# Graph attention block: softmax arguments in natural node order, a new step order, and the division of P shared by ScalarE and VectorE

## The reference

```python
h = relu(layernorm(x))
# 4 heads, then one more "back" head on the concatenated heads
Wh = h @ W[head];  f1 = Wh @ a1;  f2 = Wh @ a2
e  = leaky_relu(f1[:, None] + f2[None, :], 0.01)
e  = where(adj > 0, e, -1e9)
attn = softmax(e, axis=-1)
h_head = elu(attn @ Wh)
...
y = ffn(out) + out;  x = x + layernorm(y) * gamma + beta
h = relu(layernorm(x))
x = x + deg * (h @ Wi + b) + adj @ (h @ Wj)
```

## Time and profile before

| | us |
|---|---|
| median of 3 runs | 1514.7 (1514.22 to 1515.41) |
| profiled execution: time | 1505.55 |
| its span in the trace | 1503.5 |
| busy: TensorE matmuls | 1339.4 |
| busy: VectorE | 1190.4 |
| busy: ScalarE | 1083.5 |
| busy: GpSimd | 349.2 |

### The profile page before, as it was taken

The page is one execution under the profiler, slowest core; times in us unless marked ns, Lnnn a source line. Parts: engine busy times, 40 slices in busy tenths (PEclk is TensorE's granted clock), DMA queues, the critical chain, the costliest instruction groups (busy, mean ns, idle before and its releaser), DMA issues.

```text
span 1503.5 us, 27090 instructions
## 1 busy us (share of the span) xinstructions
PE 1339.4 (89%) x9944; PEld 1260.0 (84%) x9944; DVE 1190.4 (79%) x2833; ACT 1083.5 (72%) x2037; POOL 349.2 (23%) x234
## 2 busy tenths in 40 slices
...
DMA packets 53091, 54.07 MB, mean 36 GB/s; under 512 B 14048, under 2 KB 41696, under 8 KB 52832
## 3 DMA queue, kind: packets, MB, share of 16 engines
...
## 4 chain that ended last, share of the span: by engine, by line
PE 51%; DVE 35%; issue 6%; ACT 5%; POOL 2%; DMA 2%; POOLq 0%; ACTq 0%; DVEq 0%; SPq 0%
PE ps L747 33%; DVE arg L625 12%; PE ps L780 5%; DVE prob_lo L606 4%; DVE arg L653 4%; PE ps L830 4%; PE ps L871 4%; PE ps L840 3%; DVE elu L661 2%; DVE zneg L633 2%; DVE whx_lo L606 2%; DVE st L587 1%; POOL hx_lo L378 1%; DVE xb L699 1%; PE ps L849 1%
## 5 line engine op out<-in xcount | busy, mean ns | idle before, releaser
L378 POOL TENSOR_TENSOR hx_lo<-elu,hx_hi 128x512 fp32r<-128x512 f32 x128 | 171.2, 1338 | 622.7 <-ACT hx_hi L474 622.7
L747 PE MATMUL ps<-prob_hi,whx_hi 128*128 128x256 f32 x1024 | 298.5, 291 | 11.4 <-DVE wk L661 7.6
L747 PE MATMUL ps<-prob_lo,whx_hi 128*128 128x256 f32 x1024 | 289.7, 283 | 0.0
L747 PE MATMUL ps<-prob_hi,whx_lo 128*128 128x256 f32 x1024 | 289.2, 282 | 0.0
L625 DVE CUSTOM_DVE_ANT_0 arg<-f2bc,mask 128x512 f32<-128x512 f32 x320 | 278.7, 907 | 1.9 <-DMA f2bc<-f_rows 1.6
L444 ACT ACTIVATE arg<-arg,nmax 128x512 f32<-128x512 f32 x320 | 227.7, 718 | 0.6 <-DVE nmax L636 0.5
L440 ACT ACTIVATE arg<-arg,fcol 128x512 f32<-128x512 f32 x320 | 213.5, 721 | 12.1 <-DVE gmax L625 12.1
L780 PE MATMUL ps<-ident,arg 128*128 128x128 f32 x1280 | 186.9, 290 | 36.9 <-DVE arg L653 32.4
L747 PEld LDWEIGHTS ps<-prob_hi,whx_hi 128*128 128x128 f32 x1024 | 196.1, 192 | 17.2 <-issue 9.7
L780 PEld LDWEIGHTS ps<-ident,arg 128*128 128x128 f32 x1280 | 170.6, 209 | 45.0 <-DVE arg L653 34.8
L450 ACT ACTIVATE prob_hi<-ps 128x1024 fp32r<-128x1024 f32 x160 | 163.4, 1021 | 58.7 <-PE ps L747 33.1
...
## 6 DMA issues: line engine op xcount, KB each, us to landing
...
f_rows<-fcol SPq DMA_DIRECT2D x80, 2.0 KB, 3.4
...
```

Of the source, the lines that this page charges most:

```text
L378: pool.tensor_tensor(out=hx[1][:, 2 * c.h:2 * c.h + 2, c.u * HN:(c.u + 1) * HN], in0=elu[:, c.buf, :, :], in1=hx[0][:, 2 * c.h:2 * c.h + 2 ...
L747: i = pe.matmul(out, a, b_, start=(k == 0), stop=(k == n - 1))
```

## The change

Three things. The mask is made in natural node order by one instruction over all four row tiles; rowmax reads f2bc with a step of four floats and writes arg in natural order; turn_p reads contiguous blocks. `scale` is split: ScalarE multiplies row tile 0 of a unit (new semaphore p_scaled0, on which turn_p waits too), VectorE row tile 1. All five step tables are in a new order, in which ScalarE's has the ten new `scale` entries.

```diff
-            for n in range(NC):
-                i = dve.tensor_scalar(mask[:, n, :].rearrange("p (q c) -> p c q", c=NC), adj_f[:, n, :].rearrange("p (c q) -> p c q", c=NC),
-                                      0.0, 1.0, ALU.is_gt, ALU.mult)
-            i.then_inc(s_adj, 1)
+            dve.tensor_scalar(mask[:, :, :], adj_f, 0.0, 1.0, ALU.is_gt, ALU.mult).then_inc(s_adj, 1)
...
+            def scale(c):
+
+                act.wait_ge(rinv_made, c.unit + 1)
+                act.activation(arg[:, c.abuf, 0, :], arg[:, c.abuf, 0, :], ACT.Copy, scale=rinv[:, c.abuf, 0:1]).then_inc(p_scaled0, 1)
...
-                    dve.tensor_tensor_reduce(out=arg[:, c.abuf, n, :], in0=f2bc[:, head % F2S, :], in1=mask[:, 2 * c.u + n, :],
+                    dve.tensor_tensor_reduce(out=arg[:, c.abuf, n, :].rearrange("p (c q) -> p c q", c=NC),
+                                             in0=f2bc[:, head % F2S, :].rearrange("p (q c) -> p c q", c=NC),
+                                             in1=mask[:, 2 * c.u + n, :].rearrange("p (c q) -> p c q", c=NC),
...
-                for n in range(2):
-                    i = dve.tensor_scalar(arg[:, c.abuf, n, :], arg[:, c.abuf, n, :], rinv[:, c.abuf, n:n + 1], None, ALU.mult)
-                i.then_inc(p_scaled, 1)
+                dve.tensor_scalar(arg[:, c.abuf, 1, :], arg[:, c.abuf, 1, :], rinv[:, c.abuf, 1:2], None, ALU.mult).then_inc(p_scaled, 1)
...
             def turn_p(c):
+                pe.wait_ge(p_scaled0, c.unit + 1)
                 pe.wait_ge(p_scaled, c.unit + 1)
...
-                        i = pe.transpose(p[:, j, n, :], arg[:, c.abuf, n, :].rearrange("p (q c) -> p c q", c=NC)[:, j, :], ident[:, :])
+                        i = pe.transpose(p[:, j, n, :], arg[:, c.abuf, n, j * P:(j + 1) * P], ident[:, :])
```

More of the change, by code:

```diff
@@ L12 @@
 PE_STEPS = [
[L13 to L17, removed]
@@ L20 @@
+    ("turn_p", 1, 1), ("turn_in", 0, 0), ("ffn1", 0, 3), ("turn_gc", 0, 4), ("attend", 0, 1), ("attend", 1, 1),
+    ("turn_p", 2, 1), ("conv_in", 0, 4), ("m1", (0, 0), 0), ("conv_in", 1, 4), ("turn_p", 3, 1), ("m1", (0, 1), 0),
+    ("ffn2", 0, 3), ("attend", 2, 1), ("turn_p", 4, 2), ("attend", 3, 1), ("conv", 0, 4), ("m1", (1, 0), 0),
+    ("turn_p", 5, 2), ("m1", (1, 1), 0), ("turn_p", 6, 1),
 ]
 ACT_STEPS = [
-    ("probs", 4, 3), ("norm_ff_out", 0, 4), ("elu_neg", 3, 2), ("hx", 2, 2), ("elu_exp", 3, 2), ("probs", 5, 3),
@@ L23 @@
[L23 to L26, removed]
-    ("elu_neg", 9, 2), ("m1", (3, 0), 1), ("elu_exp", 9, 2), ("hx", 9, 2), ("norm_in_out", 0, 0), ("args", 0, 1),
@@ new lines @@
+    ("elu_exp", 8, 2), ("m1", (2, 1), 1), ("turn_out", 0, 3), ("hx", 8, 2), ("norm_in_out", 0, 0), ("elu_neg", 9, 2),
+    ("m1", (3, 0), 1), ("elu_exp", 9, 2), ("args", 0, 1), ("m1", (3, 1), 1), ("hx", 9, 2), ("scale", 0, 1), ("args", 1, 1),
+    ("probs", 0, 1), ("scale", 1, 1), ("norm_gc_out", 0, 4), ("mix2", 0, 2), ("args", 2, 1), ("mix2", 1, 2), ("probs", 1, 1),
+    ("turn_in", 0, 0), ("args", 3, 1), ("turn_gc", 0, 4), ("scale", 2, 1), ("ffn1", 0, 3), ("elu_neg", 0, 1),
+    ("scale", 3, 1), ("elu_exp", 0, 1), ("elu_neg", 1, 1), ("elu_exp", 1, 1), ("probs", 2, 1), ("hx", 0, 1),
@@ L33 @@
+    ("elu_neg", 6, 1), ("elu_exp", 5, 2), ("elu_exp", 6, 1), ("probs", 8, 1), ("scale", 9, 1),
 ]
 DVE_STEPS = [
-    ("m1", (1, 1), 3), ("elu_out", 5, 5), ("probs", 7, 4), ("rinv", 9, 4), ("scale", 9, 4), ("elu_out", 6, 4),
-    ("probs", 8, 4), ("m1", (2, 0), 3), ("elu_out", 7, 4), ("m1", (2, 1), 3), ("rowmax", 0, 3), ("probs", 9, 4),
-    ("elu_out", 8, 4), ("rowmath", 0, 3), ("norm_gc", 0, 6), ("rowmax", 1, 3), ("rowmath", 1, 3), ("rowmax", 2, 3),
-    ("elu_out", 9, 4), ("rowmath", 2, 3), ("m1", (3, 0), 3), ("mix2", 0, 4), ("rinv", 0, 3), ("scale", 0, 3), ("rinv", 1, 3),
```

53 lines of the change are left out of this document (30 added, 23 removed).

## The result

The changed kernel takes 1543.08 us (median of 4 runs, 1535.9 to 1552.12), the kernel before 1514.46 beside it. The ratio is 1.0192, with a 95% interval from 1.0144 to 1.0241. The forecast was 1489 us.

A forecast was written before the change was run, and what follows sets the result against it. Bounds: TensorE for most of the round, VectorE in the 22 us behind conv. 81.5 + 3.5 = 85.0 us a round, 23.9 saved over 12.85 rounds, 26 with start and end: 1479.6 profiled, 1489 from the median; range 1453 to 1536.

The forecast's parts named there:

- The prices: Costs of the changed instructions: rowmax plus 0.40 us, transposes minus 0.8 us a round, ScalarE's half 0.72 us a unit.
- hx_lo: TensorE's wait at mix2, directly after the attend it depends on; the new order was to remove it, minus 1.7 us a round.
- With VectorE's idle time down from 13.9 to some 8.5 us a round I leave 3.5 us of waits.: TensorE's waits per round under the new order: 3.5 us, the 2.9 already there for VectorE plus 0.6 new.
- GpSimd's losses come on top: Behind conv, VectorE's time lost to GpSimd adds to its 17.1 us of work, so part of 2.9 us of waits stays.
- rowmax 8 waits for turn_p 5 likewise, 0.6 us: In VectorE's new queue, rowmax 8 needs turn_p 5 first; VectorE was to idle 0.6 us there.
- Start and end: Before and after the steady rounds: cheaper mask, earlier first division, dearer rowmaxes, unchanged end; together minus 2 us.
- VectorE as the bound: Rival, chance 0.15: VectorE keeps 5 us idle a round; slower once d, one rowmax's added price, passes 0.67 us; 1534 us.
- ScalarE late: Rival, chance 0.10: turn_p waits for ScalarE's half of the division; at 0.3 us a unit about 1527 us.
- A wash: Rival, chance 0.13: rowmax's added price is 0.53 us and VectorE returns most of what the order removes; 1512 us.
- Nearly all waits removed: Rival, chance 0.12: VectorE's stretch behind conv vanishes too, 1.1 us of waits stay, round 82.6 us; 1458 us.

The follow-up runs named there:

- e6: The changed kernel with rinv 8, scale 8 and probs 6 moved in front of rowmax 9 in VectorE's table; 1511.95 us, ratio 1.0016 to the kernel before.
- e7: The changed kernel with GpSimd's gamma and beta applied to row tile 0 alone, so its output is not the reference's; 1493.22 us, ratio 0.9881.
- e2: The kernel before with the new step order alone: old arithmetic, cheap rowmax, no split division; 1513.83 us, ratio 1.0036.
- e4: The changed kernel with mask, rowmax and turn_p as before: new order, split division, cheap rowmax; 1505.39 us, ratio 0.9987.
- e8: e4 with probs 6 moved in front of rowmax 9; 1472.85 us, ratio 0.9768.
- e11: e2 with probs 6 moved in front of rowmax 9 (cheap rowmax, no split division); 1491.82 us, ratio 0.9915.
- e12: e8 with GpSimd's three 128x1024 instructions each cut into four of 128x256; 1471.43 us, ratio 0.9743.

## Why the prediction was wrong

**The prices.** Right. Rowmax: 0.41 us more for 0.40. Transposes: eight take 0.87 to 0.89 us, and all of the ten rounds 104.7 us in e6 for 113.9 before, 0.9 us a round for 0.8. TensorE's work at a granted clock of 1.00 is 81.46 a round (e6) for 81.5; that it fits so well is in part luck, since e7, with the same matmuls and the same clock, has 81.00. ScalarE's half takes 0.715 us for 0.72, and no wait of TensorE in the ten rounds is for it. VectorE busy 75.6 a round for 76.5, ScalarE 74.0 for 73.4. The mask in one instruction takes 1.23 us, 1.2 saved for 0.6.

Of the price of rowmax the Trainium skill (Vector Engine (DVE) Microarchitecture Reference, "Measured stream behaviour on trn2") gives 1.73 ns for 1.054 a column when one source hops 4 KiB at every element, an estimate of 0.35 us; here, with a step of 16 bytes, it is 0.41 us for 512 elements, 0.80 ns each. The rule speaks against the edit with reason, and its figure is a little low for this step in this instruction.

**hx_lo.** Right: that wait is gone in e2 and in after.

**"With VectorE's idle time down from 13.9 to some 8.5 us a round I leave 3.5 us of waits."** This is the step that failed, and it failed before the dear rowmax came in. Even with the cheap one the new order has 4.74 us of waits (e2). The step compared sums: 17.1 us of VectorE's work between conv and elu_out 7 against 17.9 of TensorE's. A sum says nothing about which step stands in front of which. Read in order, the same table that gave 17.1 us has rowmax 8, probs 5 and rowmax 9 in front of probs 6, while TensorE has only turn_p 7 and attends 4 and 5 left to do, and is through with them 7.4 us after attend 4 begins (614.57 to 625.17 less 3.23). It then also had "GpSimd's losses come on top" without placing them; in the round shown 5.0 us of them fall into the 14.4 us before probs 6 is done. e6 (move the step: 24.9 to 0.3 us) and e7 (shorten GpSimd: 24.9 to 5.9) show both halves of the cause. And "rowmax 8 waits for turn_p 5 likewise, 0.6 us" was seen and measured at 0.77, but what stands behind it, the copy of m1 (1, 0) for which attend 4 waits 1.76 us, was not followed.

**The clock.** Not in the forecast. Of the 4.16 us a round between 85.0 and 89.16, 3.0 are waits (6.51 for 3.5) and 1.1 is TensorE's busy time (82.64 for 81.5), which goes with the lower granted clock behind the wait at attend 6. Over ten rounds that is 41.6 us of the 72.5 by which the profiled execution (1552.12) misses the forecast for it (1479.6); the medians miss by 54.

**Start and end.** Forecast at minus 2 together. In the profiled executions the sixth load went out 17.5 us later than before (303.08 for 285.56), and the part behind the ten rounds is 6.3 us longer (355.66 for 349.34), which is what its 2.85 rounds make at 2.3 us more each; the end itself is as it was. The order has most of the 17.5: the load is 11.6 us late in e2 (297.17) and 9.0 in e4. Between 66 and 303 us the granted clock is 0.93 in after, where it was 0.98 up to the sixth load before. One turn_p waits 13.8 us there, behind VectorE's one-time preparation of weights, where the longest such wait was 10.6 before. Up to the sixth load TensorE waited 9.8 us for ScalarE's half (four times, up to 4.9), a wait that the ten rounds don't have; before, it waited 26.5 us there for VectorE's division, so the 9.8 are no added cost by themselves. What in the new order delays the start was not tried and stays open. The sum: 17.5 + 23.0 + 6.3 = 46.8 us, the 1550.3 of span for 1503.5, with the 18 us in it that come from which execution was profiled.

**The rivals.** *VectorE as the bound* gives the right sign, and its mechanism is false. It supposed a floor of 5 us of idle time and a switch at d = 0.67. The loss came at d = 0.41 with 13.6 us idle, and e6, at the same price and with less idle time (86.19 less 74.4, 11.8 us), takes before's time. VectorE is late at a few places of its queue, attend 6 above all, and not full. *ScalarE late* is refuted for the steady rounds: no wait for it there, and the split gains 0.5% (e4 against e2) to 1.5% (e8 against e11). *A wash* had the mechanism nearest to what happened, the dear rowmax giving back what the order removes, but only for a price of 0.53 and a gain of the order that didn't exist. *Nearly all waits removed* (1.1 us of waits, a round of 82.6) didn't happen in any kernel; e8 and e12 come nearest, with 2.3 and 2.0 us of waits and 84.13 and 83.79 a round, once probs 6 is moved and rowmax stays cheap.

A slower kernel had a chance of 0.26, and the range ended at 1536, 7 us short of the median. It lacked a case in which a wait moves instead of going away: e2's own time, with after's price on top.
